# Attention scores from 32-row products with rows scattered by DMA, and a new order of work on four engines

## The reference

```python
h = jnp.einsum('bni,io->bno', x, W).reshape(x.shape[0], x.shape[1], H, D)
...
e_i = jnp.einsum('bhnd,hd->bhn', h, a1)
e_j = jnp.einsum('bhmd,hd->bhm', h, a2)
e = e_i[:, :, :, None] + e_j[:, :, None, :]
e = jnp.where(e > 0, e, LRELU_SLOPE * e)
e = jnp.where(adj[:, None, :, :] > 0, e, NEG_INF)
attn = jax.nn.softmax(e, axis=-1)
out = jnp.einsum('bhnm,bhmd->bhnd', attn, h)
```

## Time and profile before

| | us |
|---|---|
| median of 3 runs | 708.86 (708.76 to 709.89) |
| profiled execution | 708.05 |
| its span in the trace | 705.9 |
| first_layers, from the start to the first h_parts of gru_layer | 332.6 |
| gru_layer, the rest | 373.3 |

### The profile page before, as it was taken

How to read it: one execution, slowest core, us unless ns; L and a number is a source line. 1 busy time by engine, 2 the same in 40 slices (tenths; PEclk the granted TensorE clock), 3 DMA queues, 4 the chain that set the end, 5 groups by cost and what they waited for, 6 DMA issues and landing times.

```text
span 705.9 us, 13197 instructions
## 1 busy us (share of the span) xinstructions
PE 660.1 (94%) x4380; PEld 430.2 (61%) x4380; DVE 601.6 (85%) x1360; ACT 524.4 (74%) x962; POOL 401.1 (57%) x357
## 2 busy tenths in 40 slices
PE   3899999999999999974899999999999999999995
PEld 2678888888888888752455555555555545545552
DVE  3777877777877777666699999999999999999996
ACT  2678888888888888723588888777787777777774
POOL 4656666666666666521255555555555555555554
PEclk9999999999999999985899999999999999999998
DMA  5111111111111100000333333333333334333332
GB/s 154 31 32 31 31 32 31 32 32 31 31 31 31 31 17 2 2 0 2 64 65 64 62 61 60 74 73 68 71 62 74 75 75 75 61 76 73 68 70 74
DMA packets 114690, 35.82 MB, mean 51 GB/s; under 512 B 87680, under 2 KB 114624, under 8 KB 114624
## 3 DMA queue, kind: packets, MB, share of 16 engines
q1 hardware_dynamic: 113424, 34.79, 23.0%
q10 hardware_dynamic: 1200, 0.20, 0.2%
HBM read 9.80 MB, written 4.19 MB: 20 GB/s over the span
## 4 chain that ended last, share of the span: by engine, by line
DVE 36%; issue 10%; PE 3%; POOL 2%; ACT 1%; DMA 0%; DVEq 0%; POOLq 0%; SPq 0%
DVE h_parts L1297 12%; DVE cand L1304 7%; DVE t_parts L1289 6%; DVE r L1308 5%; DVE new L1293 4%; PE psum L50 3%; POOL h0T L1264 2%; DVE out L1280 2%; DMA h_nodes<-h_parts 0%; DVE h_parts L1299 0%; DVEq L1307 0%; ACT cand L1241 0%; POOLq L1046 0%; ACT t_parts L1233 0%; PE psum L1193 0%
## 5 line engine op out<-in xcount | busy, mean ns | idle before, releaser
L50 PE MATMUL psum<-h_parts,gru_w 128*128 128x512 f16 x720 | 185.1, 382 | 6.3 <-DVE out L1280 3.9
L1264 POOL TENSOR_TENSOR h0T<-cand,zh 128x512 f32<-128x512 f32 x80 | 101.6, 1270 | 143.4 <-DVE cand L1304 143.4
L50 PE MATMUL psum<-t_parts,gru_w 128*128 128x512 f16 x720 | 181.5, 379 | 0.0
L50 PEld LDWEIGHTS psum<-h_parts,gru_w 128*128 128x128 f16 x720 | 69.8, 98 | 91.9 <-issue 10.8
L1258 POOL TENSOR_TENSOR zh<-z,h0T 128x512 f32<-128x512 f32 x80 | 101.7, 1271 | 25.8 <-ACT z L1236 25.8
L50 PEld LDWEIGHTS psum<-t_parts,gru_w 128*128 128x128 f16 x720 | 66.9, 98 | 66.4 <-DVE t_parts L1289 2.9
L1233 ACT CAST t_parts<-psum 128x512 f16<-128x512 f32 x80 | 46.8, 585 | 72.6 <-PE psum L50 72.6
L1297 DVE CAST h_parts<-h0T 128x512 f16<-128x512 f32 x80 | 90.1, 1126 | 4.9 <-PEq L380 4.8
L578 POOL TENSOR_TENSOR prob<-prob,row_max 128x512 f32<-128x512 f32 x64 | 68.7, 1086 | 20.0 <-DVE row_max L956 18.7
L1241 ACT ACTIVATE cand<-new,gates_b 128x512 f32<-128x512 f32 x80 | 65.0, 812 | 7.4 <-DVE new L1293 7.3
L1236 ACT ACTIVATE z<-psum,gates_b 128x512 f32<-128x512 f32 x80 | 62.2, 778 | 5.9 <-PE psum L50 0.9
(11 more groups left out here) (131 smaller groups left out, 1202.5 us busy)
## 6 DMA issues: line engine op xcount, KB each, us to landing
x_all<-in_x SPq DMA_DIRECT2D x16, 256.0 KB, 3.2
adj<-in_adj SPq DMA_DIRECT2D x16, 256.0 KB, 2.8
out_x<-out SPq DMA_DIRECT2D x16, 256.0 KB, 2.3
h_nodes<-h_parts SPq DMA_TRANSPOSE x80, 3.1
gw<-in_L_gnn_weight SPq DMA_DIRECT2D x1, 320.0 KB, 5.7
W<-in_L_gnn_W SPq DMA_DIRECT2D x2, 128.0 KB, 4.4
wi<-in_L_gnn_w_ih SPq DMA_DIRECT2D x1, 192.0 KB, 5.7
wh<-in_L_gnn_w_hh SPq DMA_DIRECT2D x1, 192.0 KB, 4.4
```

The source lines that it names most:

```text
L50: return nc.tensor.matmul(out, lhsT, rhs, start=start, stop=stop)
L1264: pool.tensor_tensor(state(now), by_graph(cand[now.s][:, :]), by_graph(zh[now.s][:, :]), ALU.add)\
```

## The change

Six things change in `first_layers`; `gru_layer` stays as it is.

- The score terms of a group are four products, one per graph, of 32 columns of weights each (`score_w` is 128 x 32), put into the four 32-row strips of one 128 x 128 area of bank 4. `keep_e` and `keep_e_lo` work on 128 x 128 elements instead of 128 x 512 and 32 x 512. A scalar per row decides what each row gets, so that e_parts holds, for each graph, rows of high and low parts and rows of ones.
- The e_j rows are scattered into a second operand, `spread` (two buffers), by eight DMAs for each group, issued by SP: each takes four rows of 128 16-bit numbers, one from each graph's strip. `spread_e` waits for `keep_e_lo`. It stands ahead of the load of x of the group two later.
- `scores` is one product per graph, 32 rows deep and 512 columns wide. It waits for the DMAs. The mask products of all four graphs stand ahead of it in a function of their own (`mask`), with the transposes of `adj` between.
- `pick_i`, `pick_j` and their making on POOL go; DVE makes three row scalars from the identity by four small instructions and ACT fills the two `spread` buffers, all at the start.
- `find_gone` moves from slot N to slot N+1, between `divide` and `add_attended`.
- The order on PE, ACT, DVE and POOL is new, and the last layernorm's normalising, its transpose and copy come one slot later (`at(4)`), so that there are slots with `at(4)` and one more slot at the end.

```diff
-        for row in (0, LO_ROW):
+        for row in (0, 2 * HEADS):
...
+            def spread_e(group):
+
+                sp.wait_ge(score_weights.picks, 2)
+                sp.wait_ge(e_lo, group.count)
+                if group.before(2).exists:
+                    sp.wait_ge(e_landed[group.odd], group.before(2).spreads)
+                    sp.wait_ge(score_ready, group.before(2).graph_count(GROUP - 1))
+                for h in range(HEADS):
+                    for part in range(2):
+                        sp.dma_start(spread[group.odd][16 + part * HEADS + h::ROWS, h, :],
+                                     e_parts[group.odd][(2 * part + 1) * HEADS + h::ROWS, :])\
+                            .then_inc(e_landed[group.odd], 16)
...
-                mm(nc, P[:, B_EDGE, :], t["score_w"][:, :], hT[:, :]).then_inc(e_psum, 1)
+                for g in range(GROUP):
+                    last = mm(nc, P[g * ROWS:(g + 1) * ROWS, B_E, 0:NODES], t["score_w"][:, :],
+                              hT[:, g * 128:(g + 1) * 128])
+                last.then_inc(e_psum, 1)
...
-                mm(nc, bank, e, t["pick_i"][:, :, :], False, False)
-                for h in range(HEADS):
-                    last = mm(nc, bank[:, h, :], t["pick_j"][:, h, :], e, False, h == HEADS - 1)
-                last.then_inc(score_ready, 1)
+                pe.wait_ge(e_landed[group.odd], group.spreads)
+                for g in range(GROUP):
+                    rows = slice(g * ROWS, (g + 1) * ROWS)
+                    mm(nc, P[:, g, :].rearrange("p (h m) -> p h m", h=HEADS), e_parts[group.odd][rows, :],
+                       spread[group.odd][rows, :, :], False, True).then_inc(score_ready, 1)
...
-                if at(2):
-                    add_self(at(2))
+                if at(4):
+                    normalise(at(4), 3)
+                if at(0):
+                    normalise(at(0), 0)
                 if at(3):
                     bias(at(3), 1, t["b3"])
-                if at(0):
-                    normalise(at(0), 0)
...
-                if at(3):
-                    normalise(at(3), 3)
+                    less_max(at(1), 3)
+                    add_self(at(1))
```

More of the change, by code:

```diff
@@ L279, in __init__ @@
         self.ones = sb("ones", [1, 128])
+        self.row = sb("row", [128, HEADS])
         self.loaded = sem("score_weights_loaded")
         self.eyes = sem("identities_made")
+        self.rows = sem("rows_made")
         self.picks = sem("picks_made")
@@ L306, in identities, with sum_rows, pick_rows @@
                                pattern=[[-1, 128]], channel_multiplier=1).then_inc(self.eyes, 1)
-    def pick_rows(self, pool):
-        links = 3
-        for pick, row in ((self.t["pick_i"], 0), (self.t["pick_j"], HEADS)):
-            pool.memset(pick[:, :, :], 0.0).then_inc(self.glink, 1)
-            links += 1
-            for part in (0, LO_ROW):
-                pool.wait_ge(self.glink, links)
-                pool.affine_select(out=pick[:, :, :], in_=pick[:, :, :], compare_op=ALU.not_equal, fill=1.0,
-                                   base=-(row + part), pattern=[[-1, HEADS], [0, 128]],
-                                   channel_multiplier=1).then_inc(self.glink, 1)
-                links += 1
-        pool.wait_ge(self.glink, links)
-        pool.sem_inc(self.picks, 1)
+    def sum_rows(self, dve):
+        v, n, t = self.nc.vector, 2 * HEADS, self.t
+        dve.wait_ge(self.eyes, 2)
+        by_row = t["ident"][:, :].rearrange("p (g q k) -> p g q k", g=GROUP, q=ROWS // n)
+        v.tensor_reduce(self.row[:, :], by_row[:, :, 0:2, 0:HEADS].rearrange("p g q k -> p k g q"), AXIS.XY, ALU.add)\
+            .then_inc(self.rows, 1)
+        v.tensor_reduce(t["lo_rows"][:, :], by_row[:, :, 1, :], AXIS.XY, ALU.add).then_inc(self.rows, 1)
+        v.tensor_reduce(t["one_rows"][:, :], by_row[:, :, 2:4, :].rearrange("p g q k -> p g (q k)"), AXIS.XY, ALU.add)\
+            .then_inc(self.rows, 1)
+        dve.wait_ge(self.rows, 3)
+        v.tensor_tensor(t["lo_rows"][:, :], t["one_rows"][:, :], t["lo_rows"][:, :], ALU.subtract)\
+            .then_inc(self.rows, 1)
+    def pick_rows(self, act):
+        act.wait_ge(self.rows, 4)
+        for spread in self.t["spread"]:
+            self.nc.scalar.copy(spread[:, :, :], self.row[:, :].unsqueeze(2).to_broadcast([128, HEADS, 128]))\
+                .then_inc(self.picks, 1)
     def turn_max(self, pe):
@@ L398, in first_layers @@
         hT = one("hT", [128, COLS])
-        e_parts = two("e_parts", [128, COLS], F16)
+        e_high = one("e_high", [128, NODES], F16)
+        e_parts = two("e_parts", [128, NODES], F16)
         hW = two("hW", [128, GROUP, HEADS, HEAD_DIM + 1])
@@ L431, in first_layers @@
         e_lo = sem("e_lo")
+        e_landed = [sem(f"e_landed{s}") for s in range(2)]
         hW_psum = sem("hW_psum")
@@ L555, in _ @@
                 load(p, False)
+            for q in range(2):
+                spread_e(Group(GROUPS // 2, q, 2))
         @block.gpsimd
@@ L584, in normalise @@
                 wait_apart(var_ready[n], group.count)
-                if n == 0 and group.before(1).exists:
-                    wait_apart(yT_psum, group.before(1).count)
+                if group.before(1).exists:
+                    wait_apart(yT_psum if n == 0 else h0T_psum, group.before(1).count)
                 pool.tensor_tensor(y[n][:, :, :], xs(group), mean_var[n][:, :, 0:1].to_broadcast([128, GROUP, DIM]),
@@ L814, in keep_e @@
                 act.wait_ge(e_psum, group.count)
-                if group.before(2).exists:
-                    act.wait_ge(score_ready, group.before(2).graph_count(GROUP - 1))
-                a.copy(e_parts[group.odd][:, :], P[:, B_EDGE, :]).then_inc(e_hi, 1)
+                if group.before(1).exists:
+                    act.wait_ge(e_lo, group.before(1).count)
+                a.activation(e_high[:, :], P[:, B_E, 0:NODES], ACT.Identity, bias=t["one_rows"][:, 0:1])\
+                    .then_inc(e_hi, 1)
             def keep_hW(group):
@@ L879, in slot @@
                 if at(1):
+                    exponential(at(1), 0)
                     leaky(at(1), 3)
-                    exponential(at(1), 0)
                     exponential(at(1), 1)
@@ L1027, in slot @@
                     gru.keep_fused(dve)
+                if at(1):
+                    row_max(at(1), 3)
+                    keep_probT(at(1), 1)
                 if at(0):
                     keep_e_lo(at(0))
-                if at(1):
-                    keep_probT(at(1), 1)
                 if at(2):
                     add_out(at(2), 0, B_TURN)
+                    moments(at(2), 2, x_added[0], at(2).count)
+            score_weights.sum_rows(dve)
             slots(dve, slot)
```

168 lines of the change are left out of this document (84 added, 84 removed).

## The result

The changed kernel takes 727.18 us (median of 4 runs, 725.39 to 730.76), the kernel before in the same comparison 708.97: a ratio of 1.026, 95% interval 1.022 to 1.030. The forecast was 713.4 with a range of 700 to 725: the sign was right, the time 14 us too low and outside the range.

The account below looks back on a forecast made before the run. The prediction took a ring through DVE, ACT and PE (18.02 us a turn), not PE, as the bound. 708.05 + 4.0 (start) + 0.2 (ring) + 0.4 (last slot) = 712.65 profiled, so 713.4 median, range 700 to 725.

Parts of the forecast that it names:

- The ring: Chain through DVE, ACT and PE from one `add_attended` to the next, 18.02 us a turn; forecast +0.01 us a slot.
- hid: Ring's part up to ACT's hidden layer, with one `leaky` moved behind the factor: -0.06 us a slot, bounds -0.3 and +0.5.
- `gone`: `find_gone` on DVE, now between division and sum, partly beside a POOL instruction: +0.70 us a slot, bounds 0.42 and 1.21.
- `shift`: DVE's `shift` 2 falls between POOL's two y3 instructions, 0.25 us instead of 0.88: -0.63 a slot, bounds -0.72 and +0.3.
- rival 3: `shift` is caught by y3's second instruction on POOL: +0.9 us a slot, 726 us in all; chance 0.13.
- The start: First slots, where nothing covers the eight DMAs: first `leaky` at 22.1 instead of 18.00, +4.0 us, bounds +2 and +7.8.
- DMAs in steady slots: Eight issues need 6.1 us within 8.4 us of cover: cost 0, unless an issue takes over 0.81 us.
- Rival 4: The DMAs come late in each slot, at 1.0 us per issue +20 us, 733 us in all; chance 0.07.
- The last slots: Last slot with a mask behind it, where PE's floor rises from 17.27 to 17.7 us: +0.4 us.
- Rivals 1 and 2: 1: PE is the bound after all, 699.7 us, chance 0.20; 2: POOL's gap is better than taken, 708.2 us, chance 0.15.
- Rival 2: In the ring, `shift` takes 0.16 us and `gone` 0.42: -0.36 us a slot, 708.2 us in all; chance 0.15.

Follow-up runs that it names:

- e6: The kernel before with POOL's `add_self` moved behind `normalise` of layernorm 0: 702.27 us, ratio 0.991; repeated 703.34 us, 0.993.
- e4: The kernel before with only the strips, 32-row score products and eight DMAs, in the old order of all engines: 718.24 us, ratio 1.012.
- e3: The kernel before with only `find_gone` moved between division and attention sum, one slot later: 726.94 us, ratio 1.026.
- e1: The changed kernel with `find_gone` back in slot N: 721.03 us, ratio 1.018 against the kernel before.
- e12: The changed kernel with PE's order of the kernel before, all other engines as changed: 722.00 us, ratio 1.019 against the kernel before.
- e13: The changed kernel with 512-column filler products in all PE waits of slots 0 and 1: 722.55 us, ratio 1.020 against the kernel before.
- e9: The changed kernel with `out_1` moved on PE from behind the y0 transposes to ahead of the adj transposes: 746.72 us, ratio 1.054.

## Why the prediction was wrong

**Reading of before: right.** The ring binds and PE does not. e6 shows it by shortening one DVE step, with PE's work as it was; e4 by taking work from PE, with no shorter turn. e3, which lengthens DVE, fits but would fit a full PE too.

**hid, forecast -0.06, measured -0.23.** Better than I took it, and inside its bounds.

**`gone`, forecast +0.70, measured +0.61** (e1: 0.54). Right in mechanism, duration 0.82, and place: inside POOL's first y0 instruction, ending 0.29 us after it, as in the earlier trace rows.

**`shift`, forecast -0.63, measured +0.15.** This is the step that failed in the ring. I let DVE slip through a gap of 0.15 us between y3's two instructions. Counted from the end of the last sum (127.36), the gap was at 13.71 to 13.86 and DVE came at 13.89. It missed by 0.03 us. My own sum had errors of 0.17 us for DVE (14.06 forecast) and 0.29 for POOL's second instruction (14.15 forecast): each larger than the gap. That is rival 3, which I gave 0.13 because it needed DVE "later than 14.15"; what it needed was either engine off by a tenth. I should have given it about even odds. It alone is 0.78 a turn, 12 x 0.78 = 9.4 us of the 14. That rival 3's total of 726 lies so near the measured 727 is luck: its turn was 18.9, not 18.55, and it had nothing for the clock.

**The clock, not in the forecast.** This is the second step that failed, a term left at nothing without a reason: I foresaw that PE would wait one to two us a slot, and still priced all of its work at the clock of the kernel before. What goes with the stretches at 1.2 GHz is 4.8 us for PE's order (e12) and 4.3 for the waits at the start (e13). With `shift` that makes 18.5; hid and `gone`, 0.26 a turn better than forecast, give back 3.1, and the cheaper scattering below 1.7. That leaves 13.7 of the 13.8 missed; the closeness says little, since each part is known to a us at best.

**The start, forecast +4.0.** The first `leaky` was forecast at 22.1 and came at 20.41: low parts ready at 14.07 instead of 15.5 (I had not scaled the score product, 0.66 us instead of 2.05, nor the smaller tiles of ACT and DVE), issues at 0.55 instead of 0.49 each, and the last row used at most 1.8 us after its issue began, not 2.7. I also left out that `gone`, made a slot later, holds up the first masks by 1.97 us; it costs next to nothing only because the rows land no earlier (score products at 19.89, with `gone` early in e1 at 19.84). To the end of the first turn the profile is 4.3 later, in its repetition 8.3: the number is near, its parts were wrong, and the clock made up the difference.

**DMAs in steady slots, forecast 0: right.** Eight issues take 4.28 us, 0.535 each, under the threshold of 0.81; PE never waits for them. Rival 4 is out.

**The last slots, forecast +0.4**: +0.17 in the next to last turn; the last depends on the clock. In e12, with no stretch there, the last two turns are 17.30 and 17.24, before 17.32 and 17.27: the +0.4 isn't there.

**Rivals 1 and 2.** PE was relieved by more than I said (1.2 us of busy time a slot, in e4 1.5) and nothing came of it. Rival 2's `shift` of 0.16 would have needed the missed gap.

## What to carry to other kernels

When two engines hold each other up as DVE and POOL do here, an instruction of 0.16 us costs the rest of the instruction that it falls on (here up to 1.03 us), so a forecast that depends on a gap narrower than its own error is a coin toss and belongs into the chances as one. Before taking work from an engine, find who ends the ring: here one moved line on POOL gave 0.7 to 0.9%, and the work taken from PE gave no shorter turn, not even with that line moved (17.67 against 17.52). Where contention is cleared from one step, look where it goes: it went to the other `shift`. And PE's order is a price of its own even where PE is not the bound: the same products in another order ran with no stretch at half the clock (e12), some (the changed kernel) or one in nearly each turn (e9).

## What I had not expected of the hardware

- The granted clock fell to 0.50 although PE never idled for more than 1.62 us at a time in the steady part (e9) and, in the changed kernel, was 100% busy for 3 us directly ahead of the stretch at 197 us. It depends on the order of the products (e12: none; e9: nearly each turn). What exactly the chip answers to stays open.
- The same kernel has these stretches in other places in each execution, and nearly the same time: 725.4 and 726.8 us in the two profiled.
- In the first slots of e4 and e12 PE works at half speed up to 38 us while the column of the granted clock shows 1.00; durations of known products (5.17 against 2.77 us) tell it, the column doesn't.
- 32-column fp32 products into four column strips also run together: eight records of 128 columns in 0.43 us, where the two of 512 columns in the kernel before took 1.08 in a steady slot.
